# The causal mask of the row maxima, added on TensorE instead of VectorE, and both PSUM pairs taken at once

## The reference, cut to what matters

```python
q1 = _split_heads(x @ Wq1, H)     # H = 16 heads of 32 columns
q2 = _split_heads(x @ Wq2, H)
k = _split_heads(x @ Wk, H)
v = _split_heads(x @ Wv, H)
q = jnp.concatenate([q1, q2], axis=1)
k2 = jnp.repeat(k, 2, axis=1)
scores = jnp.einsum('bhqd,bhkd->bhqk', q, k2) * scale
causal = jnp.tril(jnp.ones((T, T), dtype=bool))
scores = jnp.where(causal, scores, jnp.finfo(scores.dtype).min)
p = jax.nn.softmax(scores, axis=-1)
y = jnp.einsum('bhqk,bhkd->bhqd', p, v2)
y = y1 - sigmoid(x @ Wlam) * y2   # y1 from the heads of q1, y2 from those of q2
```

## Time and profile before

| | |
|---|---|
| median of three runs | 2149.65 us |
| the three runs | 2146.57, 2151.14, 2149.65 us |
| the profiled execution | 2146.57 us |
| its span, first to last instruction | 2144.8 us |
| mean granted TensorE clock, share of full | 0.988 |
| PE busy | 2054.2 us, 96% |
| DVE busy | 1378.3 us, 64% |
| ACT busy | 855.2 us, 40% |
| POOL busy | 889.0 us, 41% |

### The profile page before, as it was taken

The page is one execution under the profiler, slowest core; times in us unless marked ns, Lnnn a source line. Parts: engine busy times, 40 slices in busy tenths (PEclk is TensorE's granted clock), DMA queues, the critical chain, the costliest instruction groups (busy, mean ns, idle before and its releaser), DMA issues.

```text
span 2144.8 us, 28629 instructions
## 1 busy us (share of the span) xinstructions
PE 2054.2 (96%) x11312; PEld 885.8 (41%) x11312; DVE 1378.3 (64%) x2094; ACT 855.2 (40%) x1304; POOL 889.0 (41%) x459
## 2 busy tenths in 40 slices
PE   7999999999999998999999999999999998899999
PEld 3444444444444444343434333343433333444444
DVE  5868687657755645666666666666667823675634
ACT  4434344334444323334343434343344442443431
POOL 3757585500000001676766565766756682000000
PEclk9999999999999999999999999999999988999999
DMA  7110011300000020000001010000000111000001
GB/s 230 35 35 30 30 35 32 140 0 1 1 1 1 1 62 11 2 16 16 16 11 21 11 21 1 16 16 16 1 11 6 43 47 40 0 1 20 20 1 40
DMA packets 68997, 55.48 MB, mean 26 GB/s; under 512 B 36800, under 2 KB 55232, under 8 KB 68608
## 3 DMA queue, kind: packets, MB, share of 16 engines
q1 hardware_dynamic: 61952, 41.07, 6.7%
q10 hardware_dynamic: 6912, 12.59, 1.8%
HBM read 43.02 MB, written 10.62 MB: 25 GB/s over the span
## 4 chain that ended last, share of the span: by engine, by line
PE 53%; DVE 4%; ACT 3%; POOL 2%; issue 1%; DVEq 0%; ACTq 0%; POOLq 0%
PE psum L116 9%; PE psum L1152 9%; PE psum L1240 8%; PE psum L1264 7%; PE psum L1294 6%; PE psum L140 5%; PE psum L1190 3%; POOL b_totals L1521 2%; PE psum L1277 2%; PE psum L1252 2%; PE psum L1198 1%; PE psum L1270 1%; DVE b_maxima L1588 1%; DVE psum L1586 1%; ACT b_probs L1440 1%
## 5 line engine op out<-in xcount | busy, mean ns | idle before, releaser
L1521 POOL TENSOR_TENSOR b_totals<-b_totals,b_probs 128x2048 f32<-128x2048 f32 (+3 forms) x160 | 515.7, 3223 | 323.4 <-ACT b_probs L1440 312.8
L1588 DVE TENSOR_REDUCE b_maxima<-psum 128x2 f32<-128x1024 f32 (+3 forms) x384 | 362.9, 958 | 127.0 <-PE psum L1240 117.4
L1440 ACT ACTIVATE b_probs<-psum 128x1024 f32<-128x1024 f32 (+3 forms) x320 | 228.3, 765 | 275.2 <-PE psum L1277 174.9
L435 PE MATMUL psum<-hT,a_win 128*128 128x512 f32 x640 | 290.8, 597 | 0.8 <-ACT hT L555 0.8
L116 PE MATMUL psum<-hT,b_early 128*128 128x512 f16 x1024 | 226.9, 381 | 6.9 <-DVE b_middle L202 6.9
L116 PE MATMUL psum<-hT,W 128*128 128x512 f16 x1024 | 226.5, 381 | 3.9 <-DVE a_win L202 3.9
L1586 DVE TENSOR_TENSOR psum<-psum,b_row_mask 128x256 f32<-128x256 f32 x256 | 109.3, 427 | 185.7 <-PE psum L1240 185.7
L435 PEld LDWEIGHTS psum<-hT,a_win 128*128 128x128 f32 x640 | 119.4, 191 | 129.4 <-issue 128.2
L116 PEld LDWEIGHTS psum<-hT,b_early 128*128 128x128 bf16 x1024 | 100.0, 98 | 132.1 <-DVE b_middle L202 9.3
L116 PEld LDWEIGHTS psum<-hT,W 128*128 128x128 bf16 x1024 | 100.6, 98 | 126.4 <-DVE a_win L202 7.6
L1495 POOL MEMSET b_mask<- 128x128 f32 x1 | 0.2, 204 | 356.9 <-POOLq L267 356.9
(11 more groups left out here) (226 smaller groups left out, 3338.0 us busy)
## 6 DMA issues: line engine op xcount, KB each, us to landing
a_parts<-in_w_guT ACTq DMA_DIRECT2D x32, 256.0 KB, 2.8
ternary<-W SPq DMA_DIRECT2D x1, 6144.0 KB, 18.1
a_win<-in_w_inT SPq DMA_DIRECT2D x20, 256.0 KB, 7.3
a_parts<-in_w_pT ACTq DMA_DIRECT2D x16, 256.0 KB, 2.7
b_down<-lam_rows SPq DMA_DIRECT2D x32, 128.0 KB, 2.8
b_early<-ternary SPq DMA_DIRECT2D x8, 512.0 KB, 8.2
out<-x SPq DMA_DIRECT2D x16, 256.0 KB, 2.2
x<-in_x SPq DMA_DIRECT2D x3, 1024.0 KB, 8.0
```

What stands on the lines that cost most here:

```text
L435: last = pe.matmul(ring(s, j), win[:, at:at + P], core["hT"][:, (i * KT + k) * BLK:(i * KT + k + 1) * BLK], start=(k == 0), stop=(k == KT ...
L1440: act.activation(held(u, s)[:, 2 * a:2 * a + 2, off:BLK], pair_banks(("score", u, s, a))[:, :, off:BLK], ACT.Exp, scale=SCALE).then_inc(ex ...
L1521: pool.tensor_tensor(acc, acc, held(u, s)[:, :, off:BLK], ALU.add).then_inc(summed, 1)
L1588: dve.tensor_reduce(maxima[u % 2][:, :].rearrange("p (h q c) -> p h q c", h=HPT, q=QT)[:, 2 * a:2 * a + 2, qt, kc], pair_banks(("row", u, ...
```

## The change

1. `row_mask` goes: its tile, its memset and its select on GpSimd, and the mask addition with its `settle` on VectorE (line 1586).
2. In a diagonal row pass TensorE adds the mask: after the four score matmuls of the pass, four matmuls of 128 x 128 in bf16 with `later_key` as weights and `ident_b` streamed, into the last 128 columns of each head (`start=False`). The semaphore that VectorE waits for, `row_done`, is now raised by the mask matmuls.
3. In `row` and in `scores`, both pairs are taken before the first matmul. Before, the second pair was taken between the matmuls of the second and the third head.

```diff
-        row_mask = sb("row_mask", P)
...
-                width = hi - kc * BLK
-                to = []
+                width, diagonal = hi - kc * BLK, kc == qt // TPB
+                to = [take_pair(("row", u, n, a)) for a in range(2)]
                 for j in range(HPT):
-                    if j % 2 == 0:
-                        to.append(take_pair(("row", u, n, j // 2)))
                     last = pe.matmul(to[j // 2][:, j % 2, 0:width], strip(qT[w][r % 2], j, qt * P, (qt + 1) * P),
-                                     strip(kT[w][r % 2], j, kc * BLK, hi), start=True, stop=True)
-                    if j % 2:
+                                     strip(kT[w][r % 2], j, kc * BLK, hi), start=True, stop=not diagonal)
+                    if j % 2 and not diagonal:
                         last.then_inc(row_done, 1)
+                if diagonal:
+                    for j in range(HPT):
+                        last = pe.matmul(to[j // 2][:, j % 2, width - P:width], later_key[:, :], ident_b[:, :],
+                                         start=False, stop=True)
+                        if j % 2:
+                            last.then_inc(row_done, 1)
...
-                to = []
+                to = [take_pair(("score", u, s, a)) for a in range(2)]
                 for j in range(HPT):
-                    if j % 2 == 0:
-                        to.append(take_pair(("score", u, s, j // 2)))
                     pe.matmul(to[j // 2][:, j % 2, off:BLK], strip(kT[w][r % 2], j, kt * P, (kt + 1) * P),
...
             pool.memset(mask[:, :], 0.0).then_inc(pconst, 1)
-            pool.memset(row_mask[:, :], 0.0).then_inc(pconst, 1)
-            pool.wait_ge(pconst, 2)
-            pool.affine_select(out=row_mask[:, :], in_=row_mask[:, :], compare_op=ALU.is_ge,
-                               fill=-3e38, base=0, pattern=[[-1, P]], channel_multiplier=1).then_inc(pconst, 1)
+            pool.wait_ge(pconst, 1)
...
-            dve.wait_ge(pconst, 4)
+            dve.wait_ge(pconst, 2)
...
                     dve.wait_ge(row_done, (u * NR + n) * 2 + a + 1)
-                    if kc == qt // TPB:
-                        own = pair_banks(("row", u, n, a))[:, :, width - P:width]
-                        v.did(dve.tensor_tensor(own, own, row_mask[:, :].unsqueeze(1).to_broadcast([P, 2, P]), ALU.add))
-                        v.settle()
```

## The result

The changed kernel takes 2173.88 us (median of four runs, 2168.71 to 2177.26), the kernel before 2149.63 beside it: 1.0109 times as long (95% interval 1.0088 to 1.0132), so by the medians 24 us slower. The forecast was 12 us slower, and 2173.88 lies above its range. The profiled execution took 2175.0 us, its span is 2172.1, its granted clock 0.984 in the mean.

What follows compares the result with a forecast made beforehand. TensorE, busy 2054 of 2145 us, was taken as the bound. Lead 0.7, unit 0 2.4, unit 1 0.3, units 2 to 12 8, unit 13 0.6, end -0.2 gave about +12: 2161.5 us on the median, range 2152 to 2171.

Steps and rivals of the forecast that it cites:

- the paragraph on what is moved: Row and score passes: taking both pairs first costs score passes nothing, but delays a row pass's first pair and DVE.
- one wait a period: Step 3 of even units: the score pass waits 0.4 us for maxima after the late row pass of step 2.
- The ends: Outside the steady period: unit 0 +2.4 us, from unit 13's step 5 onward -0.2.
- the clock: Lead, 815 to 832 us, partly at the lower clock: a few us of full clock worth some 2 us either way.
- The mask matmuls: Diagonal row passes: four added matmuls cost 0.33 us, 42.2 us over 128 passes if none is covered.
- The low bound of 0.22: Four mask matmuls in a row pass: 0.22 us if no change of shape is paid beyond today's one.
- The waits taken back: PE waits at steps 11, 0, 1 and 6 of a two-unit period: 4.2 us regained by relieving DVE.
- Masks alone: Steady two-unit period without early taking: 16 x 0.33 us of masks less 4.2 us of waits taken back.
- the waits for the output add: Step 11, odd unit: the row pass's 1.17 us wait falls to no more than 0.1; 1.15 taken back.
- the dear case: Rival: four mask matmuls cost 0.44 us, +11 us on top, 2172 us; chance 0.10.
- The two halves of the change don't pay the same: Rival: early taking delays row passes more than one wait a period; stays under the dear case; no separate chance.
- Cheap: Rival: four mask matmuls cost 0.22 us, -11 us, so +1, 2151 us, no measurable change; chance 0.12.

Runs made afterwards that it cites:

- after: The changed kernel itself, mask on TensorE and both pairs taken early, against the kernel before: 2173.88 us, 1.0109.
- e1: Changed kernel, but each second bank pair is taken between the second and third head, as before; mask stays on TensorE: 0.9997 of the kernel before.
- e6: Changed kernel with the two waits at the head written in the other order, second pair first, in row and score passes: 2154.23 us.
- e4: e1 with both pairs taken at the head in score passes only: 4.7 us over the kernel before.
- e3: e1 with both pairs taken at the head in row passes only: 17.1 us over the kernel before.
- e5: e1 with TensorE masking only row passes 0, 1 and 2 of a unit (steps 10, 11, 0), VectorE the rest: 2132.82 us, 0.9932 of the kernel before.
- e10: Kernel before, mask on VectorE, both pairs taken at the head of each pass, the second pair's wait written first: 2164.20 us.
- e7: Kernel before with one more long-met wait behind the first pair's in every row and score pass; nothing taken earlier: 2149.55 us.
- e8b: e1 with four more matmuls of the same shape, zero weights, ahead of the masks: 28.0 us over e1 by the medians.
- e2: Kernel before, mask on VectorE, with both pairs taken at the head of row and score passes: 1.0131 of the kernel before.

## Why the prediction was wrong

**The failed step.** It is the paragraph on what is moved: "In a score pass this costs nothing", and in a row pass one wait a period, 0.4, and 1.3 in unit 0. Measured beside the masks (after against e1) the early taking costs 2.46 a period and, by the medians, some 25 us in all. By its parts:
- The delay as such: e6 against e1, 0.83 a period. The 0.40 at step 3 of the even unit is there. Beside it steps 2 and 3 of the odd unit and steps 4 and 5 of both lose and gain 0.3 to 0.4 each and nearly cancel (4 and 5 in e6: +0.33 and -0.32 even, +0.33 and -0.12 odd). The same pairs stand in e4 and not in e3, so they are the score passes'. Their loss is given back a step later, all but 0.2 a period: the argument that all four heads end at the later wait plus one pass was right in the main for the score pass, once the order of the waits is set aside.
- The order of the waits: 1.63 a period. No sentence of the forecast considers that two waits can't both stand on the weight load, and which of them is late. I counted waits, and not the instructions that carry them, so this term stood at nothing.
- The ends: unit 0 was 7.4 for 2.4, unit 14 and what follows 3.0 for -0.2. In unit 0 2.7 are the clock and some 1.0 the order of the waits (e6, without either: 3.7). From unit 14 on e6 comes to -0.4, near the forecast. The forecast allowed 2 us for the clock either way; it had the place wrong, the lead and not unit 0.

**Terms with another size, in the other direction.** The mask matmuls were taken at 0.33 and cost 0.19 in place, but for the 0.33 of step 5: 14 x 0.19 + 2 x 0.33 = 3.3 a period where 5.3 were forecast. The low bound of 0.22, no change of shape beyond today's, was the right value; the 0.33 of the earlier trace rows holds only in front of narrow weights, those of `weigh` and of the denominators. I had also counted the changes of shape wrongly. Before, a row pass (32 rows) is followed by a fill of 128 x 128; now the masks of 128 x 128 stand between them, and the number of changes between 32 rows and 128 is the same. One more change, from 128 x 128 to 128 x 32, comes only in step 5, and there the masks cost 0.14 more than elsewhere. The Trainium skill, TensorEngine Tiling (Array Packing), section Tiling Modes, says that a change of tiling mode drains TensorE; the rows agree with it so far as they go (0.19 without a further change of mode, 0.33 with one), but no run here shows a drain by itself. The waits taken back were 4.2 by forecast. In e5 the six masks that count shorten the period by 2.13 and cost 6 x 0.19 = 1.1 themselves, so 3.3 came back. Masks alone were forecast at +1.1 a period and came to +0.02 (e1). Had the early taking cost what I said, the kernel would have been at 2148.3 + 6.6 x 0.4 + 1.3 = 2152; two errors of opposite sign made the forecast look nearer than its parts were. That it missed by no more than 12 us is in part luck.

**What held.** DVE's 1269 us; 512 matmuls of 219 ns; the direction of the waits for the output add, 0.3 at the most instead of 1.17, where 0.1 was forecast; the waits for the maxima at the score pass of step 0, which are gone in the period (at step 1 PE still idles 0.12 in both units); the relief too small to win with all masks moved; unit 13 at +0.6, as forecast, and unit 1 at -0.1 for 0.3. The period, forecast at 122.7, was 123.66.

**The rivals.** "The two halves of the change don't pay the same" is what happened. I had it inside the dear case with the argument that ScalarE frees the bank within 0.25 us in all but two row passes a period. That bounds the delay of the release and says nothing of the 0.09 behind it, which falls due at every late pass. "Cheap" was right on the masks and wrong on the time.

Open: what makes the clock fall in unit 0 in some runs and not in others, and the lead's part, which moved between 0.7 and 5.3 us in these kernels without an order that I could read; and unit 14, which grew by 2.9 us in the changed kernel, 0.6 in e1, 2.4 in e6 and 5.3 in e10.

## What to carry to other kernels

Where a pass waits for two semaphores, write first the wait that will be met last, so that it stands on the weight load (worth 14 us here with the mask on VectorE, and 17 with it on TensorE, 2.7 of these by way of the clock), and take nothing earlier than it is used. Work moved from a waited-for engine to the bound one paid only where that engine's queue was late: here 3 of 8 masks won 0.7%, all 8 nothing. Time each half of a two-part change by itself.

## What the runs showed of the hardware

- A wait that is long met costs TensorE nothing, even as an instruction of its own, 383 times (e7: 1.0005, interval 0.9997 to 1.0014). A late one costs 0.08 to 0.09 us more on an instruction of its own ahead of the weight load than on the weight load (after and e6).
- Four bf16 matmuls of 128 x 128, on full rows between 32-row fp32 passes and 128-row fp32 fills, take 0.23 to the next work, 0.19 net; four more of them 0.22 (e8b). Where weights of 32 columns follow they take 0.33 (e1, step 5).
- Taking both pairs at the head makes TensorE less busy and the kernel slower. e2 has the 11312 matmuls of the kernel before, 1997.0 us with one in flight instead of 2054.2, and takes 29 us longer: a pass that ran in two halves, with a wait between them, counted as busy in part of that wait.
